# The causal attention and top-2 expert block of a fused model: four loops of one pair each become one course, with 32-row key products and masks that open the banks of scores

## What is computed

```python
z = layernorm(x)
q, k, v = split(z @ w_qkv)            # 16 heads of 8 features
s = q @ k.T / sqrt(8), causal         # 256 x 256 for each head
z = z + softmax(s) @ v @ w_o
h = layernorm(z) * g1 + b1
w = softmax(h @ wg); keep the two largest of 8, normalised
y = sum over 8 experts e: w[e] * (gelu(h @ w1[e] + bb1[e]) @ w2[e] + bb2[e])
x = x + layernorm(h + y) * g2 + b2
```

## Time and profile before

| what | value |
|---|---|
| median of 3 runs | 6051.03 us (6046.5 to 6054.4) |
| the profiled execution's own time | 6044.81 us |
| its span in the trace | 6043.0 us |
| granted clock, mean | 0.885 |
| PE busy | 5056.1 us (84%) |
| DVE, ACT, POOL busy | 2937.1, 2132.9, 581.6 us |
| the changed block, in the span | 4297 to 5067 us |

### The profile page before, as it was taken

The page is one execution under the profiler, slowest core; times in us unless marked ns, Lnnn a source line. Parts: engine busy times, 40 slices in busy tenths (PEclk is TensorE's granted clock), DMA queues, the critical chain, the costliest instruction groups (busy, mean ns, idle before and its releaser), DMA issues. The chain is left out here.

```text
span 6043.0 us, 116717 instructions
## 1 busy us (share of the span) xinstructions
PE 5056.1 (84%) x47039; PEld 3296.6 (55%) x47299; DVE 2937.1 (49%) x9864; ACT 2132.9 (35%) x4169; POOL 581.6 (10%) x1312
## 2 busy tenths in 40 slices
PE   4489999999999984988888889898689887887784
PEld 3266666666666653555455545554456554655553
DVE  6534444444444442677667767766322332334333
ACT  2232222222222221566566656665222222222121
POOL 2300000000000013111111111111000000000000
PEclk7699889989989986999999999999789888888885
DMA  0100000000000012000000000000000001000000
GB/s 23 30 8 2 2 2 2 2 2 2 2 2 2 2 37 60 9 4 9 4 8 4 9 4 8 4 8 1 36 1 1 1 1 39 1 1 1 1 1 8
DMA packets 33024, 51.25 MB, mean 8 GB/s; under 512 B 8445, under 2 KB 23959, under 8 KB 31842
## 3 DMA queue, kind: packets, MB, share of 16 engines
q1 hardware_dynamic: 29154, 39.66, 2.1%
q10 hardware_dynamic: 2304, 2.11, 0.1%
q0 software_dynamic: 1024, 1.78, 0.1%
HBM read 39.02 MB, written 4.19 MB: 7 GB/s over the span
## 5 line engine op out<-in xcount | busy, mean ns | idle before, releaser
L1157 PE MATMUL psum<-g_still,ident_bf 128*128 128x512 bf16 (+6 forms) x3128 | 943.8, 349 | 75.5 <-issue 73.5
L2277 DVE TENSOR_REDUCE l_m<-psum 128x2 bf16<-128x512 f32 x768 | 503.7, 692 | 167.9 <-PE psum L1881 164.9
L1157 PEld LDWEIGHTS psum<-g_still,ident_bf 128*128 128x128 bf16 x3388 | 409.2, 139 | 143.4 <-issue 83.7
L2153 ACT ACTIVATE l_probs<-psum,l_mcol 128x1024 f32<-128x1024 f32 x384 | 406.3, 1109 | 177.3 <-PE psum L1919 177.3
L1881 PE MATMUL psum<-l_kb,l_qmb 32*128 32x256 bf16 x1536 | 299.6, 277 | 71.1 <-DVE l_m L2277 52.2
L1237 ACT ACTIVATE g_th<-g_pre 128x256 f32<-128x256 f32 x512 | 191.5, 417 | 349.9 <-DVE g_pre L1270 349.9
L1919 PE MATMUL psum<-l_qm,l_keys 32*128 32x256 f32 x3072 | 269.6, 424 | 14.5 <-issue 14.5
L1270 DVE TENSOR_TENSOR g_pre<-g_encp,psum 128x256 f32<-128x256 f32 x512 | 192.8, 418 | 168.8 <-PE psum L1188 122.0
L1945 PE MATMUL psum<-l_probs,l_v 128*32 128x256 f32 x3072 | 224.2, 413 | 46.2 <-DVE l_o L2317 28.7
L2164 ACT COPY l_heads_out<-psum 128x256 f32<-128x256 f32 (+1 forms) x292 | 130.0, 445 | 370.3 <-PE psum L1945 187.0
L2277 DVE TENSOR_REDUCE l_cm<-psum 128x4 bf16<-128x256 f32 x400 | 166.2, 427 | 178.3 <-PE psum L1881 178.2
(11 more groups left out here) (569 smaller groups left out, 10723.5 us busy)
## 6 DMA issues: line engine op xcount, KB each, us to landing
s_w<-in_S_w SPq DMA_DIRECT2D x16, 256.0 KB, 5.2
f_w<-in_F_w SPq DMA_DIRECT2D x2, 2048.0 KB
l_wf<-in_L_W SPq DMA_DIRECT2D x7, 576.0 KB, 3.8
l_w<-in_L_W SPq DMA_DIRECT2D x1, 3072.0 KB, 10.1
l_wc<-in_L_W SPq DMA_DIRECT2D x7, 384.0 KB, 2.9
l_nw<-in_L_nw SPq DMA_DIRECT2D x1, 2304.0 KB, 7.9
l_wa<-in_L_W SPq DMA_DIRECT2D x7, 320.0 KB, 2.8
h_w<-in_H_W ACTq DMA_DIRECT2D x16, 129.0 KB, 3.0
```

Of the source, the lines that this page charges most:

```text
L1157: pe.matmul(psum[:, bank, 0:cols], cst["ident_bf"][:], still[:, 0:cols], start=True, stop=True)
L2153: act.activation(probs[:, u % 2, chunk, :].rearrange("p (g n) -> p g n", g=GROUP), psum[:, 0:GROUP, S * chunk:S * chunk + S], ACT.Exp, bia ...
L2277: dve.tensor_reduce(place, psum[:, c.bank(("max", u, g)), 0:x.tiles * x.width] .rearrange("p (t k) -> p t k", t=x.tiles), AX.X, ALU.min)\
```

## The change

The pass that was run four times by a loop becomes one pass with everything written out: the first part is attention for all 32 units, the second the experts for all 32 combinations of pair and expert. What belongs to a neighbouring pair (norm statistics, transposition, projections, output projection, residual) is written between the units of a pair, one piece per unit (`chain`). A pair's units are 0 to 7. The norms at the start read `x` as soon as the block begins; the expert matrices have a semaphore of their own, for which only the second part waits. The exponentials and values leave out the masked quarter (chunk 1 needs only 128 of 256 query columns). The expert biases are no longer one-row products: the weights are turned once per pair and multiplied by the 8x128 matrix of biases. The core of the diff:

```diff
+        def max_scores(u, g):
+            bank = spare_bank(("max", u, g))
+            pe.matmul(psum[:, bank, :], cst["neg_ident"][:], causal[:], start=True, stop=False)
+            for t in range(2):
+                cols = P * (t + 1)
+                last = pe.matmul(psum[:, bank, S * t:S * t + cols], qmb[group(g), n % 2, j, ...],
+                                 kb[group(g), n % 2, S * b:S * b + cols], start=False, stop=t == 1)
+        def masks(u):
+            if u: pe.wait_ge(sig["probs_ready"], 2 * u)
+            for g in range(GROUP):
+                pe.matmul(psum[:, g, :], cst["ident_bf"][:], causalT[...], start=True, stop=False)
+        def scores(u, c):
+            if c == 0: pe.wait_ge(sig["queries_ready"], u + 1)
+            for g in range(GROUP):
+                last = pe.matmul(psum[:, g, S * c + P * c:S * c + S], keys[group(g), ...],
+                                 qm[group(g), u % 2, P * c:S], start=False, stop=c == 1)
+            if c == 1: last.then_inc(sig["scores_ready"], 1)
+        def values(u):
+            pe.wait_ge(sig["probs_ready"], 2 * u + 2)
+            if u: pe.wait_ge(sig["values_taken"], u)
...
+        for u in range(count):                       # TensorE
+            values(u - 1)
+            masks(u)
+            scores(u, 0)
+            max_scores(u + 1, 2)
+            scores(u, 1)
+            max_scores(u + 1, 3)
+            max_scores(u + 2, 0)
+            chain(p, k)
+            turn_values(u - 1)
+            turn_max(u + 1)
+            max_scores(u + 2, 1)
...
+        for u in range(count):                       # ScalarE
+            copy_values(u - 1)
+            exponentials(u, 0)
+            exponentials(u, 1)
+            chain(p, k)
...
+        for u in range(count):                       # VectorE
+            row_max(u + 1, 1); row_max(u + 1, 2); row_max(u + 1, 3); row_max(u + 2, 0)
+            chain(p, k)
+            invert_sums(u - 1)
+            normalise(u - 1)
+            place_max(u + 1)
...
+        for s in range(steps_count):                 # TensorE, experts
+            units(s + 1)
+            result(s)
+            if e == 4: ...                           # four transposes of the weights
+            if e == 5: ...                           # four products with b2
-                last = pe.matmul(out, onerow[:], b2[:, D * (e - 1):D * e], start=False, stop=True)
```

More of the change, by code:

```diff
@@ L2441 @@
 F_DH = 8
+F_UNITS = 2 * GROUP
+F_VALUES, F_MAXIMA, F_SHARED = 4, 5, 7
 def top2_block(nc, dram, X, psum, cst):
@@ L2460, in top2_block @@
[L2460 to L2469, removed]
-        rsum = sb("rsum", [P, 2, 2, GROUP])
@@ new lines, in column, with tokens, by_tile, wide @@
+        def column(name, i):
+            at = NARROW[name] + i
+            return narrow[:, at:at + 1]
+        def tokens(x, p):
+            return x[:, PT * p:PT * p + PT, :]
+        def by_tile(bank):
+            return psum[:, bank, :].rearrange("p (t d) -> p t d", t=PT)
+        def wide(col):
+            return col.unsqueeze(2).to_broadcast([P, TILES, E])
+        def unit(u):
+            n, k = divmod(u, F_UNITS)
+            return n, k // GROUP, k % GROUP
+        uses = [("max", 0, g) for g in range(GROUP)] + [("max", 1, 0), ("turn", 0, 0)]
@@ L2690, in _, with apply @@
-                    norm_vector(dve, sig, steps, "n2", lambda t: hm[:, t, :], n2, lambda t: zn[:, t, :])
-                    steps.after(affine(zn[:], zn[:], 2, 3))
-                    xall = X[:, ds(pair * PT, PT), :]
-                    dve.tensor_tensor(xall, xall, zn[:], ALU.add)
+                        last = dve.bn_aggr(n["mv"][:, t, :], n["stats"][:, t, :])
+                    last.then_inc(sig[name + "_var_ready"], 1)
+                def apply(name, n, src, dst, done):
+                    dve.wait_ge(sig[name + "_rstd_ready"], done + 1)
+                    for t in range(PT):
+                        last = dve.tensor_scalar(dst(t), src(t), n["mv"][:, t, 0:1], n["rstd"][:, t, :], ALU.subtract, ALU.mult)
+                    return last
@@ new lines, in _ @@
+                steps.after(dve.tensor_reduce(lmax[:], logits[:], AX.X, ALU.max))
+                dve.tensor_tensor(logits[:], logits[:], wide(lmax[:]), ALU.subtract).then_inc(sig["shifted_logits_ready"], 1)
+                dve.wait_ge(sig["router_exp_ready"], 1)
+                steps.after(dve.tensor_reduce(lsum[:], w_a[:], AX.X, ALU.add))
+                steps.after(dve.reciprocal(lsum[:], lsum[:]))
+                steps.after(dve.tensor_tensor(w_b[:], w_a[:], wide(lsum[:]), ALU.mult))
+                for t in range(TILES):
+                    last = dve.max(top[:, t, :], w_b[:, t, :])
@@ new lines, in _ @@
+                steps.after(last)
+                for t in range(TILES):
+                    last = dve.max_index(topi[:, t, :], top[:, t, :], w_b[:, t, :])
+                dve.tensor_tensor(pair_sum[:], top[:, :, 0], top[:, :, 1], ALU.add)
+                steps.after(last)
+                steps.after(dve.tensor_copy(topf[:], topi[:]))
+                steps.after(dve.reciprocal(pair_sum[:], pair_sum[:]))
+                numbers = number[:].unsqueeze(1).to_broadcast([P, TILES, E])
+                dve.tensor_tensor(w_a[:], wide(topf[:, :, 0]), numbers, ALU.is_equal)
```

648 lines of the change are left out of this document (465 added, 183 removed).

## The result

The changed kernel takes **5770.08 us** (median of 4 runs, 5767.08 to 5777.82) where the kernel before, timed beside it, took 6048.76 us (4 runs, 6037.25 to 6054.4): a ratio of 0.9544, 95% interval 0.9526 to 0.9561. Timed again on another occasion it was 5770.75 us for 6047.72, ratio 0.9536 (0.9519 to 0.9554). The prediction, 5802 with 5762 to 5856, lies 32 us (0.6%) too high. The profiled execution took 5767.08 us.

What follows compares the result with a forecast made beforehand. PE work bounds attention and experts, idle PE the edges. The block's terms, 25 + 209 + 3.3 + 15 + 3 + (256.0 - 3.5) + 5 + 7.3, make 520 us for 770, giving 5802 us for the kernel; range 5762 to 5856.

Steps and rivals of the forecast that it cites:

- Attention: All 32 units from first exact scores to last values: 209 us plus 3.3 to the values.
- The walk round the loop: One attention unit, values to values: first reduction after 3.0 us, three reductions to 5.2, reciprocal to 5.7, next values 5.9.
- the rival's 1.65: Attention's exact scores: four heads don't overlap in already open banks, +1.65 us a unit, 5854 us; chance 0.13.
- The rival of a shorter unit: Attention: PE hides masks and mode changes, exponentials' loop decides at 5.3 or 4.9 us; 5783, at the end 5771; chance 0.14.
- a step loses its four biases, 4 x 0.41 = 1.64 us: Expert steps: removing four one-row bias products takes each step from 9.44 to 7.80 us.
- The 5 us of low clock at the start: Start of the experts: the low clock costs 5 us, once instead of four times.
- The edges: Block start 25 us to first exact scores; last values to first gelu 15 + 3; end 7.3.
- The forecast's list: Block start: constants at 8 us, then casts, norm, transposition, projections, statistics, reductions, placing; first exact scores at 25 us.
- one pair's router with its 15 us: Turn to the experts: 15 us to the last pair's router, from 14.65 before, then 3 to the first gelu.
- The mode changes: PE switching between products over 128 and 32 rows: about 0.08 to 0.1 us each, four before a unit's first reduction.
- The low clock: Attention: the chip grants 1.2 GHz throughout, units need 11 us, experts perhaps 250 us more; 6195 us; chance 0.02.
- 6 taken: Whole kernel: the median of the runs lies 6 us above the profiled execution, turning 5796 into 5802.

Runs made afterwards that it cites:

- x2: Changed kernel with expert bias products back at full height (128 rows, all but one zero), turned weights and their products out: 5798.32 us, ratio 0.9583 to the kernel before.
- x5: Changed kernel with the four mask products of each attention unit issued twice: 5806.45 us, ratio 0.9605 to the kernel before.
- x3: Changed kernel without the masks of the exact scores, which then open their banks themselves: 5758.04 us, ratio 0.9514 to the kernel before.
- x6: Changed kernel with every head's exact scores multiplied over all 128 rows, forcing heads one behind another: 5843.6 us, one run.
- v2: Changed kernel with VectorE dividing before its last reduction and the chain, and values turned ahead of the chain: 5769.67 us, ratio 0.9536 to the kernel before.
- v3: Changed kernel with both the diagonal masks behind the scores and the values' bank taken earlier: 5755.37 us, ratio 0.9527; timed again 5743.3 us, ratio 0.9491.
- x1: Changed kernel with the one-row expert bias products back, turned weights and their products out: 5854.9 us, ratio 0.9682 to the kernel before.
- x4: Changed kernel with all four heads' keys and queries for exact scores read from group 0's 32 rows: 5913.12 us, ratio 0.9766 to the kernel before.
- x7: Changed kernel with each head's mask made from the 32 rows of its own group instead of full height: 5758.37 us, one run.
- v1: Changed kernel with masks written behind the scores, only over the diagonal's 128 columns: 5776.15 us, ratio 0.9553 to the kernel before.

## Why the prediction was right, and where it was off

**Attention was right, mechanism and size.** 212.3 forecast, 211.9 measured. That they meet within 0.4 is partly luck: x2, whose attention is the same code, took 206.5 at a granted clock of 0.98 instead of 0.95. The walk round the loop held at each stop: x5 and x3 show that the masks lie on it with their whole length (0.86 and 0.97), x6 that the four heads do overlap and what it would cost if not (1.62, the rival's 1.65), v2 that reductions and chain ahead of the reciprocal are what the next values wait for. The rival of a shorter unit fell: the exponentials end 1.1 us before the next values begin. By the total alone it would have looked right, for it ended at 5771, and 5770 was measured; the unit took 5.96 all the same, and the time came from elsewhere. That its 4.97 us can be had (v3) took another order and smaller masks.

**The mis-sized term is the bias in the experts**, "a step loses its four biases, 4 x 0.41 = 1.64 us". Measured: 4 x 0.61 = 2.44 and a step of 7.01. Over 128 biases that is 0.20 x 128 = 26 us too little saved. The 0.41 was the distance from the start of the bias record to the next tile; 0.20 more were left inside the 1.09 of the tile. The prediction even had the numbers that would have told: 1.50 from tile to tile, and 3.54 for the wide products, whose eight records of 512 columns make 0.11 for 128, so 0.89 a tile, which leaves 0.61. x1 and x2 show what the height of the product costs, 0.38 of the 0.61, on both sides of it. The 5 us of low clock at the start came as 3: 32 x 7.01, and 4 x 1.70 for the bias products of the pairs, less the 3.5 done early, make 227.6 of the 230.6.

**The edges were undersized by 9.5 us**, start 5.7 and turn 3.8. At the start the constants came 2 us later, and from the cast to the scores passed 20.7 us for 17. The forecast's list adds up to 17.9, and it has no masks in it: the approximate product and the four masks that TensorE still does behind the placing took 2.46 from its end on, and the five reductions 4.4 for 3.3, as they waited for products at the lower clock. At the turn the forecast counted one pair's router with its 15 us; there are four in a row, each waiting for its transposed tokens, 2.2 us apart, 6.6 for the three more. Part of it came back: from the last values to the first router pass 10.8 us (4537.61 to the first line below) where it was 12.9 before (4403.31 in the earlier trace rows to the second, of the kernel before).

```profile
4548.38 0.95 PE L2705 MATMUL psum<-f_wg,f_hT 128*128 128x8 f32 x8
```

```profile
4416.23 1.88 PE L2564 MATMUL psum<-f_wg,f_hT 128*128 128x8 f32 x8 [0.68 <-ACT f_hT L2596]
```

The four routers in a row were in the code: once the pass is one, what each pair did at its own end stands together at one place.

The two errors have opposite signs: -26.9 in the experts, +9.7 at the edges, -0.4 in attention, together -17.6 of the 520. That the total came as near as 32 us owes something to their cancelling. The other 14 of the 32 lie outside: 11 in and around the unchanged blocks, whose time differs by up to 16 between traces, and 3 in the step from the profiled execution to the median (6 taken, 3 measured).

**The mode changes** were right for attention (about 0.1 each: x3's 0.97 for 0.86 of x5) and too low by half in the experts (0.19). The prediction had read only the gap ahead of the first record behind a change, 0.08 to 0.1. In the experts, with 128 columns a record, as much again follows ahead of the second record; the masks (bf16, 512 columns) show 0.01 there and the values (fp32, 256 columns) 0.02. That speaks for the length of the record and not its type, but no run was made to separate them. The Trainium skill, "TensorEngine Tiling (Array Packing)", section Tiling Modes, says that a change drains the array; the gaps at both places agree with it, though no view shows the draining itself.

**The low clock** as a rival did not come true: 0.95 in attention, 0.99 in the experts. But x4 suggests that it was nearer than a chance of 2% says. The attention of a kernel that differs only in the rows from which four heads are read ran at 0.73, and took 67 us more than its full-height counterpart x6.

## What to carry to other kernels

Price a removed instruction by the distance between two like groups around it, less the groups' own records, not by the gap between its own start and the next one; the difference here was a third of its cost, 128 times. A one-row product between full-height ones pays for the change on both sides; zero-padded to full height it cost 0.23 instead of 0.61. On a loop closed by VectorE, what frees the bank that TensorE waits for belongs ahead of every reduction and norm that nobody waits for yet, and a mask belongs only over the columns where it differs from zero, behind the products that someone waits for.

## What the runs showed of the hardware

- The granted clock did not follow the busy share. In attention, x4, PE busy 97%, half of it in products of 32 rows with one group at a time: 0.73. x6, busy 91%, the same count of products, the exact scores at full height: 0.98. v2, busy 98%, with four heads side by side: 0.97. x3, busy 91%, without full-height masks: 0.85; x7, busy 87%, with the masks at 32 rows: 0.91; v1, with half their columns: 0.95. The same attention code shows 0.95 in the changed kernel, in its second profile and in x1, and 0.98 in x2, so that much is chance. x4 lies clearly outside it. x3 does in its one profile; that its missing masks are the reason is not shown, and v1 speaks rather against it. Why x4 and x6 differ stays open.
- Four 32-row products of 512 bf16 columns, each on its own row group and bank, took 0.22 us together, and 32-row fp32 products accumulate on banks opened at full height and overlap, four heads at a time (eight records in 0.65 us, against 1.73 one behind another at full height in x6).
- A change of height next to fp32 products of 128 columns: about 0.19 us each way (x1 against x2); round bf16 products of 512 columns about 0.1 (x3 against x5).
